# Turning x by a transposing DMA, from tile 5 on, in a fused long-convolution and ternary-FFN kernel

## The reference

```python
def _L0_ffn_ref(x, w_gate, w_up, w_down, ...):
    xq = int4_quant(x)                       # round(x * sqrt7 / mean|x|), clipped to -8..7
    gate = bitlinear(xq, w_gate, s_gate)     # 512 -> 1376, ternary weights
    up = bitlinear(xq, w_up, s_up)
    gate = jnp.square(jax.nn.relu(gate))
    inter = int8_quant(up * gate)
    return bitlinear(inter, w_down, s_down)  # 1376 -> 512
...
    x = x + _L0_ffn_ref(_L0_cond_ref(x, length, ...), ...)
```

## Time and profile before

| | us |
|---|---|
| three runs | 208.31, 208.82, 210.53 |
| median | 208.82 |
| the profiled execution | 209.91, of which the trace spans 207.7 |

### The profile page before, as it was taken

How to read it: one execution, slowest core, us unless ns; L and a number is a source line. 1 busy time by engine, 2 the same in 40 slices (tenths; PEclk the granted TensorE clock), 3 DMA queues, 4 the chain that set the end, 5 groups by cost and what they waited for, 6 DMA issues and landing times.

```text
span 207.7 us, 3343 instructions
## 1 busy us (share of the span) xinstructions
PE 174.6 (84%) x1072; PEld 92.9 (45%) x1089; DVE 168.5 (81%) x456; ACT 114.3 (55%) x186; POOL 10.8 (5%) x29
## 2 busy tenths in 40 slices
PE   1002679499978999999999999999999999999973
PEld 1002566345534545454454545454545454543442
DVE  6999978478988778787978897888888887879881
ACT  2186958927962727364554647382919182735630
POOL 5034502000000000000000000000000000000000
PEclk9999999969999999999999999999999999999999
DMA  2999929344899796879786968696778869755524
GB/s 64 364 384 329 315 88 321 137 159 153 157 201 220 124 226 174 219 100 242 189 204 116 245 189 167 178 194 198 149 223 138 224 143 222 105 115 126 101 73 101
DMA packets 50720, 38.31 MB, mean 184 GB/s; under 512 B 36976, under 2 KB 37312, under 8 KB 50704
## 3 DMA queue, kind: packets, MB, share of 16 engines
q1 hardware_dynamic: 49968, 36.57, 71.8%
q10 hardware_dynamic: 416, 1.47, 2.1%
q0 software_dynamic: 320, 0.06, 0.2%
HBM read 25.27 MB, written 4.28 MB: 142 GB/s over the span
## 4 chain that ended last, share of the span: by engine, by line
PE 67%; DVE 13%; ACT 9%; issue 4%; DMA 3%; SPq 2%; DVEq 0%; ACTq 0%
PE down_ps L632 16%; PE gate_ps L585 15%; PE conv_ps L500 15%; PE up_ps L590 14%; PE tr_act_ps L490 3%; DMA int_gate<-int_down 2%; DVE inter L1093 2%; ACT int_up L667 2%; ACT int_gate L674 1%; ACT int_down L667 1%; ACT int_up L674 1%; PE tr_dve_ps L555 1%; SPq L365 1%; ACT g L732 1%; DMA c_in<-in_L_cond_C_dram 1%
## 5 line engine op out<-in xcount | busy, mean ns | idle before, releaser
L590 PE MATMUL up_ps<-up_t,q_t 128*128 128x416 bf16 (+2 forms) x192 | 45.7, 361 | 0.0
L689 ACT ACTIVATE y_abs<-y 128x512 bf16<-128x512 f32 x16 | 10.1, 630 | 63.4 <-DVE y L1013 63.4
L585 PE MATMUL gate_ps<-gate_t,q_t 128*128 128x416 bf16 (+2 forms) x177 | 42.8, 360 | 1.8 <-DVE q_t L1033 1.0
L632 PE MATMUL down_ps<-down_t,i_t 128*128 128x512 bf16 (+1 forms) x164 | 37.9, 379 | 1.9 <-DVE i_t L1132 1.2
L1093 DVE SCALAR_TENSOR_TENSOR inter<-up_ps,gu_scale,g 128x416 f32<-128x416 f32 (+2 forms) x48 | 33.2, 692 | 7.5 <-issue 4.8
L500 PE MATMUL conv_ps<-toep,x_t 128*64 128x512 f32 (+3 forms) x256 | 38.2, 440 | 0.1
L732 ACT ACTIVATE g<-gate_ps,gu_scale 128x416 f32<-128x416 f32 (+2 forms) x48 | 30.3, 632 | 5.8 <-PE gate_ps L585 5.4
L1097 DVE TENSOR_REDUCE imax<-inter 128x1 f32<-128x416 f32 (+2 forms) x48 | 30.3, 631 | 1.7
L735 ACT ACTIVATE g<-g 128x416 f32<-128x416 f32 (+2 forms) x48 | 28.1, 586 | 1.5
L500 PEld LDWEIGHTS conv_ps<-toep,x_t 128*64 128x64 f32 x256 | 17.0, 138 | 23.8 <-issue 20.7
L590 PEld LDWEIGHTS up_ps<-up_t,q_t 128*128 128x128 bf16 x192 | 19.0, 99 | 18.9 <-issue 0.8
(11 more groups left out here) (179 smaller groups left out, 157.6 us busy)
## 6 DMA issues: line engine op xcount, KB each, us to landing
toep<-k_back SPq DMA_DIRECT2D x16, 512.0 KB, 4.9
x_in<-in_x_dram SPq DMA_DIRECT2D x32, 128.0 KB, 2.9
x_res<-in_x_dram SPq DMA_DIRECT2D x32, 128.0 KB, 4.0
out_dram<-o_sb SPq DMA_DIRECT2D x30, 128.0 KB, 2.4
raw_gate<-in_L_ffn_w_gate_dram SPq DMA_DIRECT2D x1, 1536.0 KB, 7.2
raw_up<-in_L_ffn_w_up_dram SPq DMA_DIRECT2D x1, 1536.0 KB, 14.0
raw_down<-in_L_ffn_w_down_dram ACTq DMA_DIRECT2D x1, 1376.0 KB, 7.1
raw_down<-in_L_ffn_w_down_dram SPq DMA_DIRECT2D x1, 1376.0 KB, 9.1
```

Source lines behind the costliest of these rows:

```text
L585: mm = pe.matmul(gate_ps[bank][:, 0:cn], q_t[p][:, i, :], gate_t[:, i, c0:c0 + cn], start=(i == 0), stop=(i == KB - 1))
L590: mm = pe.matmul(up_ps[bank][:, 0:cn], q_t[p][:, i, :], up_t[:, i, c0:c0 + cn], start=(i == 0), stop=(i == KB - 1))
L632: mm = pe.matmul(down_ps[:], i_t[0:r, c, :], down_t[0:r, c, :], start=(c == 0), stop=(c == IB - 1))
```

## The change

From tile 5 on (`X_BY_DMA` = 5) TensorE doesn't turn x. ScalarE copies the float32 words of x as two planes of 16 bits, the low and the high halves (`split_x`, 128 x 1024). SP turns both planes by one transposing DMA of eight 128x128 blocks into `xt_halves`. ScalarE then joins the turned planes to float32 words in `x_t` (`join_x`). In iteration m it joins tile m + 3 and splits tile m + 4; SP turns tile m + 4 as the last of its iteration. `x_t` becomes a pair. The residual reads the x that was loaded for the turn: `x_in` is a ring of seven, of which three and the new work tiles lie in `raw_up`, the space of the raw up weights, once these are rounded. The loads of x run up to five tiles ahead and no longer wait for TensorE; the second load of x (`x_res`) is gone.

```diff
-        x_in = [sb(f"x_in{p}", [P, L]) for p in range(2)]
-        x_res = [sb(f"x_res{p}", [P, L]) for p in range(2)]
+        x_in = [sb(f"x_in{i}", [P, L]) for i in range(4)] + [raw[1][:, i, :] for i in range(3)]
+        NX = len(x_in)
...
-        x_t = sb("x_t", [P, KB, P])
+        x_t = [sb("x_t", [P, KB, P]), raw[1][:, 5, :].rearrange("p (k t) -> p k t", k=KB)]
+        x_halves = raw[1][:, 3, :].bitcast(I16).rearrange("p (h s) -> p h s", h=2)
+        xt_halves = raw[1][:, 4, :].bitcast(I16).rearrange("p (c t) -> p c t", t=P)
...
+        X_BY_DMA = 5
...
-            def load_x(tile, p):
+            def load_x(tile):
+
+                b = tile % NX
+                if tile == 4:
+                    sp.wait_ge(w_rounded[1][0], 1)
                 for half in range(2):
-                    sp.dma_start(x_in[p][half_rows(half), :], in_dram(x, tile, half)).then_inc(x_loaded[p], 16)
+                    sp.dma_start(x_in[b][half_rows(half), :], in_dram(x, tile, half)).then_inc(x_loaded[b], 16)
...
-            def load_ahead(n, p):
-
-                sp.wait_ge(xt_turned, n - 1)
-                load_x(n, p)
+            def load_toep_free(n, p):
+
                 sp.wait_ge(conv_done, n - 1)
                 load_toep(n, p)
...
+                if k == 0:
+                    load_x(3)
+                    load_x(4)
+                if k < T - 5:
+                    load_x(m + 5)
                 if k < T - 3:
-                    load_ahead(m + 3, 1 - p)
-                if k is None or k < T:
-                    for half in range(2):
-                        sp.dma_start(x_res[p][half_rows(half), :], in_dram(x, m, half)).then_inc(res_loaded[p], 16)
+                    load_toep_free(m + 3, 1 - p)
+                if X_BY_DMA <= k + 4 < T:
+                    sp.wait_ge(x_split, m + 5 - X_BY_DMA)
+                    wait(sp, xt_copied, m + 4)
+                    sp.dma_start_transpose(xt_halves[:, :, :],
+                                           x_halves[:, :, :].rearrange("p h s -> p (h s)")).then_inc(xt_loaded, 16)
...
-                    if k < T - 2:
+                    if k + 2 < X_BY_DMA:
                         xt(m + 2, j + 1, p)
...
+            def split_x(n):
+                act.wait_ge(x_loaded[n % NX], 32 * (n // NX + 1))
+                wait(act, xt_loaded, 16 * (n - X_BY_DMA))
+                words = x_in[n % NX][:, :].bitcast(I16).rearrange("p (s h) -> p h s", h=2)
+                nc.scalar.copy(x_halves[:, :, :], words).then_inc(x_split, 1)
+
+            def join_x(n):
+                act.wait_ge(xt_loaded, 16 * (n + 1 - X_BY_DMA))
+                act.wait_ge(conv_done, n - 1)
+                words = x_t[n % 2][:, :, :].bitcast(I16).rearrange("p k (t h) -> p h (k t)", h=2)
+                nc.scalar.copy(words, xt_halves[:, :, :].rearrange("p (h c) t -> p h (c t)", h=2)).then_inc(xt_copied, 1)
...
-                elif k < T - 2:
+                elif k + 2 < X_BY_DMA:
                     xt_copy(m + 2)
+                if X_BY_DMA <= k + 3 < T:
+                    join_x(m + 3)
+                if X_BY_DMA <= k + 4 < T:
+                    split_x(m + 4)
...
-                    dve.wait_ge(res_loaded[q], 32 * (n // 2 + 1))
+                    dve.wait_ge(x_loaded[n % NX], 32 * (n // NX + 1))
...
-                                           scalar=oscale[q][:], in1=x_res[q][:, cols],
+                                           scalar=oscale[q][:], in1=x_in[n % NX][:, cols],
```

More of the change, by code:

```diff
@@ L180, in adaln_ffn @@
         w_loaded = [[sem(f"w_loaded{m}{i}") for i in range(3)] for m in range(3)]
-        x_loaded = [sem(f"x_loaded{p}") for p in range(2)]
-        res_loaded = [sem(f"res_loaded{p}") for p in range(2)]
+        x_loaded = [sem(f"x_loaded{i}") for i in range(NX)]
         toep_loaded = [sem(f"toep_loaded{p}") for p in range(2)]
@@ L213, in adaln_ffn @@
         xt_copied = sem("xt_copied")
+        x_split = sem("x_split")
+        xt_loaded = sem("xt_loaded")
         conv_done = sem("conv_done")
@@ L325, in _ @@
             load_inner(1, w_up)
-            load_x(0, 0)
-            load_x(1, 1)
+            load_x(0)
+            load_x(1)
             sp.wait_ge(zeros_ready, 1)
@@ L365, in turn_down @@
                     sp.dma_start_transpose(down_int[:, k], w_int[2][:, k]).then_inc(down_loaded[i], 16)
-            load_ahead(2, 0)
+            load_x(2)
+            load_toep_free(2, 0)
             sp.wait_ge(pads_ready, 3)
@@ L486, in xt @@
             def xt(n, j, p):
-                pe.wait_ge(x_loaded[p], 32 * (j + 1))
+                b = n % NX
+                pe.wait_ge(x_loaded[b], 32 * (n // NX + 1))
                 wait(pe, xt_copied, n)
                 for i in range(KB):
-                    mm = pe.transpose(tr_act_ps[:, i * P:(i + 1) * P], x_in[p][:, i * P:(i + 1) * P], ident[:])
+                    mm = pe.transpose(tr_act_ps[:, i * P:(i + 1) * P], x_in[b][:, i * P:(i + 1) * P], ident[:])
                 mm.then_inc(xt_turned, 1)
@@ L500, in conv @@
                         mm = pe.matmul(conv_ps[half * B:(half + 1) * B, 0:L - i * P],
-                                       x_t[:, i, half * B:(half + 1) * B], toep[p][:, half, i * P:L],
+                                       x_t[p][:, i, half * B:(half + 1) * B], toep[p][:, half, i * P:L],
                                        start=(i == 0), stop=(i == KB - 1))
@@ L684, in xt_copy @@
                 act.wait_ge(xt_turned, n + 1)
-                nc.scalar.copy(x_t[:].rearrange("p k t -> p (k t)"), tr_act_ps[:]).then_inc(xt_copied, 1)
+                if n == 1:
+                    act.wait_ge(w_rounded[1][0], 1)
+                wait(act, conv_done, n - 1)
+                nc.scalar.copy(x_t[n % 2][:, :, :].rearrange("p k t -> p (k t)"), tr_act_ps[:]).then_inc(xt_copied, 1)
+            def split_x(n):
[8 more added lines that the diff above has]
+                nc.scalar.copy(words, xt_halves[:, :, :].rearrange("p (h c) t -> p h (c t)", h=2)).then_inc(xt_copied, 1)
             def y_sum(n, p):
```

## The result

The changed kernel takes 214.57 us (median of 213.90, 214.30, 214.84 and 216.20), the kernel before 208.87 in runs beside it: a ratio of 1.025 (1.020 to 1.030). The change makes it slower by 5.7 us. Forecast were 213.2 us, in a range of 210.0 to 216.0. The execution in the profile took 214.84 us and spans 212.7, where that of before took 209.91 and spans 207.7.

A forecast was written before the change was run, and what follows sets the result against it. TensorE was taken as the bound, at a period of 9.87 us. Stall +6.8, half clock +1.6 and saved turns -4.0 gave +4.4 us on 208.82: 213.2 us, range 210.0 to 216.0.

The forecast's parts named there:

- The stall: Iteration 1: SP waits for the copy of tile 4, delaying inter_q's turn and iteration 2's down product: +6.8 us (+6.4 to +7.9).
- Rival two: First turn of x holds nothing up, only the steady gain is left: 204.8 us, faster; chance 0.07.
- The half clock: TensorE at 1.2 GHz for about 3.4 us after its idle time before iteration 2's down product: +1.6 us (0 to +2.6).
- Rival one: The stall comes without the half clock: 211.6 us, or 210.5 with full gain and short stall; chance 0.22.
- The saved turns: Iterations 3 to 13: turns of x leave TensorE, 0.36 us saved per tile, eleven times: -4.0 us (-3.5 to -4.7).
- the added turn: Steady part: SP's DMA turn of x, eight blocks, 1.25 us on SP, 3.2 us to land: no cost, covered by 0.5 us.
- Costed at nothing: Steady part: split and join, DMA turn of x, moved loads of x and dropped x_res load: 0 us.
- the cover: Steady part: 0.5 us of slack hiding the added work, gone if copies exceed about 1.3 us each or landing exceeds 4.3.
- Rival three: Added copies or queue of turns make every tile wait for i_t: +11.7 us, 220.5 us; chance 0.09.
- The signs of being wrong: No idle time at iteration 2's down product; a period of 9.8 us or more; a turn of x over 5 us.

The follow-up runs named there:

- The wait alone: Kernel before the change plus only SP's wait for xt_copied to reach 5 at the end of iteration 1, no turn behind it: 216.14 us, ratio 1.030.
- the gap filled: Changed kernel with 29 matmuls nobody reads on TensorE ahead of the down product of iteration 2: 214.02 us, ratio 1.016.
- the ring alone: Changed kernel with the ring of seven, single load of x and pair of x_t, but all turns of x on TensorE: 209.44 us, ratio 0.999.
- the doubled turns: Changed kernel without the xt_copied wait ahead of the first turn of x, each x turned twice by DMA, two extra ScalarE copies late: 214.94 us, ratio 1.024.
- the run meant to test it: Changed kernel without the xt_copied wait ahead of the first turn of x, plus 1500 already satisfied waits on GpSimd: 206.54 us, ratio 0.983.

## Why the prediction came out as it did

**The stall (+6.8; measured +6.76).** Right in place, size and cause. The chain was the one named: SP behind the copy of tile 4, then 1.34 us for the turn of x, then the turn of inter_q, then cast and down. The wait alone gave 5.30 in the kernel before, removing it gave all of the stall back. The estimate of 1.25 us on SP for eight blocks was measured at 1.25. That the two figures agree to 0.04 us is in part luck: the two issues lay 1.34 us apart, and the first product followed its cast by 0.05 us and not by 0.28. Rival two, no stall at all, didn't come.

**The half clock (+1.6, bounds 0 and 2.6; measured +2.5).** The mechanism was right, the term was mis-sized. I took the 3.4 us of one other stretch for its length; it held for 6.8 us, 5.15 of them busy. Half of 5.15 is 2.6, about the upper bound. In the experiment with the wait alone, behind a stall of 5.14 us, it held for 3.4 and cost 1.63. The rule of the Trainium skill, "TensorE: Matmul & The Clock Gate", section "Why this matters for your kernels", that the rate falls where TensorE idles between bursts, agrees with the trace both ways: with the gap filled the stretch from 78.0 to 85.0 is granted 1.00. Rival one, the stall without the half clock, is refuted by the same run.

**The saved turns (-4.0; measured -3.0 = -4.8 + 1.8).** Two errors that partly cancel. I priced the wait for the cast at 0.28 us behind its end, from one row, and took 0.36 a tile. In the clean period TensorE starts its down product 0.16 us behind the cast (174.40 + 0.52 to 175.08), at the time its own work ends, and the whole 0.44 is kept. On the other side I costed the added turn at nothing as long as that of inter_q lands within 4.3 us. The bound was about right (4.21 in a clean period) but it isn't always met: up to 5.0 us to landing in the changed kernel. That term was put at nothing against its own rows: turns landed in up to 4.4 us against 4.2 of room (4.65 - 0.43), which over eleven tiles is an estimate of up to 2 us.

**Costed at nothing.** The ring, the moved loads and the second load of x: shown to be nothing by the ring alone. The split: 1.03 us as assumed. The join: 1.33 and not 1.02, from the strided output, and just past the 1.3 us each at which I saw the cover end; the two together, 2.36, stay below. The clean periods pay nothing, but of the 0.2 us that the prediction left on SP ahead of inter_q's turn (134.2 to 134.39) 0.1 is left (170.06 to 170.16). The turn of x was put at 3.2 us to landing, by the block, and took 4.4 in the median. Rival three, a wait in every tile, didn't come; doubling the turn brings it.

**The signs of being wrong.** The prediction named three. TensorE did idle at that down product. The other two came in single iterations: a period of 9.8 or more in three of the ten (9.81, 9.85 and 10.09), and a turn of x of over 5 us once (5.6). Both belong to the term put at nothing.

**The sum.** +6.76 + 2.50 - 3.04 = +6.2 by periods; the profiled spans differ by only 5.0, as the setup came out 1.38 us shorter. The medians differ by 5.7, against a forecast of 4.4. By the periods the half clock (0.9 more) and the gain (1.0 less) would put it 1.8 to 1.9 too low and not 1.3; the rest is within the spread of the runs (213.90 to 216.20, and 208.31 to 210.53 before).

**What stays open.** What makes single periods long. What they have in common is a turn that lands late (of inter_q or of q) with the turn of x near it in SP's queue; the one execution at a period of 9.43 without the other ten turns of x has none, which points to them and doesn't show it. The every-tile wait with two turns has another mechanism, a late issue. That a fetch of instructions on q8 starts the late landings is a coincidence in most traces, which two long periods of the changed kernel contradict; the run meant to test it didn't change its number.

## What to carry to other kernels

When a loop changes its way of doing a thing in mid-run, look at the seam: a wait written for the steady state (here "the copy of the tile before is done") may, in the first iteration of the new way, point at an old-style instruction that comes much later, and all that stands behind it in a queue pays. Give the first use its own condition, and it may be none; here that is worth 8.8 us and the sign of the change. And where the slack of a transfer is tenths of a microsecond, price its slowest landing and not its median.

## What the runs showed of the hardware

- ScalarE's copy of 1024 16-bit elements to 128 partitions: 1.03 us contiguous, 1.03 with an input stride of two, 1.33 with an output stride of two. The Trainium skill, "ScalarE: Activation LUTs", section "Step-by-step: what each stage is for", gives one element per cycle and lane for every function. From 512 words at 0.61 us to 1024 elements at 1.03 it is 0.82 ns for each further element, the same with the split's strided input; the join, with as many elements, takes 0.30 us more, so for its output the rule isn't borne out.
- A DMA turn of eight blocks holds SP for 1.24 to 1.26 us where no other turn was issued just before it, and for 1.62 to 2.73 right behind another of eight blocks (the doubled turns, eleven times). The turn of inter_q, right behind that of x, held SP for 1.3 to 3.0 us in the changed kernel.
- The half clock behind idle time differs in length: 6.8 us behind a gap of 6.60 and 3.4 us behind one of 5.14. In the setup it came at about 27 us (6.8 us long) or at about 42 us (3.4 us long), or not at all, in executions of nearly the same code; down(1) then starts at 62.0 to 62.2, 63.6 to 64.9 and 61.4 to 62.9. So a setup with the late one ended 0.7 to 3.6 us later than the others; that it is the cause wasn't tested.
